# Down products of the experts, and keys, queries and values of pairs three to seven, as three products of rounded halves

## What is computed

```
x = x + tanh(g_xattn[0]) * xattn(layernorm(x), ctx, ctx, Wq, bq, Wk, bk, Wv, bv, Wo, bo)
x = x + tanh(g_ffn[0]) * ffn(layernorm(x), ...)

# xattn
q = Q @ Wq.T + bq;  k = K @ Wk.T + bk;  v = V @ Wv.T + bv      # 16 heads of 16
out = softmax(q k^T / 4) v;  return out @ Wo.T + bo
# ffn
_, topi = top_k(xf @ Wg, 2);  gates = softmax over the two chosen
for e in range(16):
    h = silu(xf @ W1[e] + b1[e]) * (xf @ W11[e] + b11[e])      # 256 -> 512
    y = y + (h @ W2[e] + b2[e]) * gates[:, e, None]            # 512 -> 256
z = silu(xf @ Ws1 + bs1) * (xf @ Ws11 + bs11) @ Ws2 + bs2      # 256 -> 1024 -> 256
```

## Time and profile before

| | us |
|---|---|
| median of 3 runs | 576.16 (576.12 to 580.23) |
| profiled execution, its own time | 570.58 |
| its span | 568.8 |
| PE busy, share of the span | 547.2, 96% |
| POOL busy | 326.7, 57% |

### The profile page before, as it was taken

One profiled execution on the slowest core, in us unless ns is written; L12 is line 12 of the kernel. 1 busy time (PEld: TensorE's weight loads), 2 busy tenths in 40 slices (PEclk: granted clock), 3 DMA queues, 4 the chain that ended last, 5 costly groups with the idle time before them and its releaser, 6 DMA issues.

```text
span 568.8 us, 11908 instructions
## 1 busy us (share of the span) xinstructions
PE 547.2 (96%) x3230; PEld 440.0 (77%) x3231; DVE 340.6 (60%) x846; ACT 238.4 (42%) x787; POOL 326.7 (57%) x267
## 2 busy tenths in 40 slices
PE   8879999999988999988999999999999999999997
PEld 6546666666657878877888888888888888888886
DVE  6556766756668853245555655566555655435687
ACT  0999899999895201202212221122212221233322
POOL 5577798898864286642375575354444650236660
PEclk9999999999999999999999999999999999999999
DMA  8671011011023145245358778557556210013442
GB/s 284 275 294 45 3 39 38 0 37 37 20 76 106 36 157 181 97 130 185 104 182 288 259 268 293 186 177 269 199 197 227 92 46 20 29 57 88 120 123 86
DMA packets 32897, 76.07 MB, mean 134 GB/s; under 512 B 4960, under 2 KB 21856, under 8 KB 29920
## 3 DMA queue, kind: packets, MB, share of 16 engines
q1 hardware_dynamic: 14960, 52.44, 26.1%
q10 hardware_dynamic: 14832, 14.82, 8.2%
q0 software_dynamic: 3072, 8.39, 4.8%
HBM read 54.93 MB, written 18.61 MB: 129 GB/s over the span
## 4 chain that ended last, share of the span: by engine, by line
PE 84%; ACT 7%; DVE 4%; issue 3%; POOL 1%; ACTq 0%; DVEq 0%; POOLq 0%
PE mid L709 14%; PE big L690 8%; PE big L692 8%; PE big L691 8%; PE big L611 5%; PE big L612 5%; PE big L613 5%; PE big L481 4%; ACT arena L797 4%; PE mid L700 4%; PE work L450 3%; PE mid L494 3%; PE work L513 3%; PE last L630 2%; PE last L506 2%
## 5 line engine op out<-in xcount | busy, mean ns | idle before, releaser
L895 ACT ACTIVATE last<-arena 128x512 f32<-128x512 f32 x47 | 28.3, 602 | 183.3 <-DVE arena L1346 183.3
L797 ACT ACTIVATE arena<-big,nmax 128x128 f32<-128x128 f32 x256 | 90.0, 388 | 3.2 <-DVE nmax L1017 3.1
L709 PE MATMUL mid<-dring,arena 128*128 x376 | 89.0, 379 | 0.0
L1346 DVE TENSOR_TENSOR arena<-big,bring 128x512 f32<-128x512 f32 x47 | 32.5, 691 | 88.9 <-PE big L692 88.9
L690 PE MATMUL big<-u_hi,xsT_hi 128*128 x188 | 81.9, 435 | 1.6 <-issue 1.6
L1509 POOL TENSOR_TENSOR u_lo<-arena,u_hi 128x2048 fp32r<-128x2048 f32 x16 | 74.3, 4642 | 1.3
L709 PEld LDWEIGHTS mid<-dring,arena 128*128 128x128 f32 x376 | 67.8, 190 | 7.3
L692 PE MATMUL big<-u_hi,xsT_lo 128*128 x188 | 73.5, 391 | 0.0
L691 PE MATMUL big<-u_lo,xsT_hi 128*128 x188 | 73.4, 391 | 0.0
L1485 POOL TENSOR_TENSOR arena<-arena,rinv 128x1024 f32<-128x1024 f32 (+1 forms) x32 | 58.6, 1832 | 23.1 <-DVE rinv L1025 23.0
L1595 POOL TENSOR_TENSOR pool_mark<-mhalf 128x1 f32<-128x1 f32 x15 | 2.9, 193 | 102.8 <-PE big L692 86.6
(11 more groups left out here) (173 smaller groups left out, 1141.2 us busy)
## 6 DMA issues: line engine op xcount, KB each, us to landing
arena<-up_w_dram SPq DMA_DIRECT2D x16, 1024.0 KB, 7.6
bring<-expert_bias_dram SPq DMA_DIRECT2D x16, 640.0 KB, 5.3
dring<-down_w_dram SPq DMA_DIRECT2D x18, 512.0 KB, 3.3
sorted_y<-arena ACTq DMA_DIRECT2D x47, 128.0 KB, 1.7
arena<-sorted_x ACTq DMA_DIRECT2D x43, 128.0 KB, 2.1
sorted_x<-dring SPq DMA_DIRECT2D x3, 1536.0 KB, 8.7
arena<-ctx_t_dram ACTq DMA_DIRECT2D x8, 256.0 KB, 2.6
dring<-up_w_dram SPq DMA_DIRECT2D x2, 1024.0 KB, 5.0
```

The source lines that it names most:

```text
L709: i = mm(mid[:, 1, 0:D], gT[:, p, c, :], dring[:, slot, c * D:(c + 1) * D], start=(c == 0), stop=(c == HC - 1))
L797: i = nc.scalar.activation(probs[:, u % 2, h, :], big[:, u % 2, h // 4, (h % 4) * CTX:(h % 4 + 1) * CTX], ACT.Exp, bias=nmax[:, u % 2, h:h ...
L1346: v.tensor_tensor(hb1[:, p, :], big[:, p, 0, :], bring[:, slot, 0:HID], ALU.add).then_inc(h1_ready, 1)
```

## The change

The down product of a block becomes twelve fp32r matmuls instead of four fp32 ones. ACT's copy now gives the rounded hidden values, and a new instruction of DVE, `keep_hidden`, the rest of them; PE waits for both. The down weights of each expert are rounded by POOL into `e_down`, with two slots, that lies over the memory of `gshT`. POOL's list for item i is now: mark and up weights as before, then a wait for the last down product of item i - 2, a second mark, and the down weights (`split_down`). Its loop is written out.

Keys, queries and values of pairs 3 to 7 become twelve fp32r matmuls each instead of four fp32 ones. Their weights are rounded once by POOL in pairs 0 and 1 (`split_projection`). The context is rounded by DVE (`round_context`, `keep_context`), the normed input too (`copy_xnT` is two instructions). The context is loaded one slot sooner, into two buffers in turn. PE turns the normed input ahead of the scores of slot 3, no longer behind them.

```diff
 
         ARENA = 16128
-        arena = sb("arena", [P, ARENA])
+        with nc.sbuf_tensor("arena", [P, ARENA], F32) as whole:
+            arena = whole
+        e_down = sb("e_down", [P, 2, 2, DCOLS], F32R)
+        gT_hi = sb("gT_hi", [P, 2, HC, P], F32R)
+        gT_lo = sb("gT_lo", [P, 2, HC, P], F32R)
+        sb("arena_rest", [P, ARENA - 4 * DCOLS - 4 * HID])
         taken = [0]
 
...
+        wr_hi, wr_lo = [u[:, 1, 0:WR].rearrange("p (w c n) -> p w c n", w=3, c=DC) for u in (u_hi, u_lo)]
+        ctx_hi, ctx_lo = [u[:, 1, WR:UCOLS].rearrange("p (c n) -> p c n", c=DC) for u in (u_hi, u_lo)]
+        xnT_hi, xnT_lo = xsT_hi[:, :, :], xsT_lo[:, :, :]
...
+            def rounded(j):
+                return not isinstance(j, int) or j >= ROUNDED
+
+            def project_rounded(w, hi, lo, done):
+                for m in range(DC):
+                    for c in range(DC):
+                        bank = work[:, m * 2 * P:(m + 1) * 2 * P]
+                        w_hi, w_lo = wr_hi[:, w, c, m * P:(m + 1) * P], wr_lo[:, w, c, m * P:(m + 1) * P]
+                        mm(bank, w_hi, hi[:, c, :], start=(c == 0), stop=False)
+                        mm(bank, w_hi, lo[:, c, :], start=False, stop=False)
+                        i = mm(bank, w_lo, hi[:, c, :], start=False, stop=(c == DC - 1))
+                i.then_inc(done, 1)
...
             def project_k(j):
-                pe.wait_ge(ctx_loaded, 16 * j + 16)
-                project(1, ctxT_1 if isinstance(j, int) and j == 1 else ctxT, k_ps, work)
+                if rounded(j):
+                    pe.wait_ge(ctx_split, j - ROUNDED + 1)
+                    project_rounded(1, ctx_hi, ctx_lo, k_ps)
+                else:
+                    pe.wait_ge(ctx_loaded, 16 * j + 16)
+                    project(1, ctxT_1 if j == 1 else ctxT, k_ps, work)
...
             def project_v(j, bank=work, halves=range(2)):
                 src = ctxT_1 if isinstance(j, int) and j == 1 else ctxT
                 for b in halves:
                     for c in range(DC):
-                        i = mm(bank[:, b * D:(b + 1) * D], src[:, c, b * CTX:(b + 1) * CTX], wqkvo[:, 2, c, :],
-                               start=(c == 0), stop=(c == DC - 1))
+                        o, rows = bank[:, b * D:(b + 1) * D], slice(b * CTX, (b + 1) * CTX)
+                        if rounded(j):
+                            mm(o, ctx_hi[:, c, rows], wr_hi[:, 2, c, :], start=(c == 0), stop=False)
+                            mm(o, ctx_hi[:, c, rows], wr_lo[:, 2, c, :], start=False, stop=False)
+                            i = mm(o, ctx_lo[:, c, rows], wr_hi[:, 2, c, :], start=False, stop=(c == DC - 1))
+                        else:
+                            i = mm(o, src[:, c, rows], wqkvo[:, 2, c, :], start=(c == 0), stop=(c == DC - 1))
...
+                    if behind and ahead2 and u == 3:
+                        pe.wait_ge(xfT_ready, j)
+                        project_xnT(j + 2)
                     if u < 2:
                         scores(j, u + 2)
                     elif ahead:
@@ -547,8 +593,8 @@
                     if ahead and behind and u == 2:
                         pe.wait_ge(qT_ready, DC * j + 2 * DC)
                         project_v(j + 1)
-                    if ahead2 and u == 3:
-                        pe.wait_ge(xfT_ready, j) if behind else pe.wait_ge(qT_ready, DC * j + 2 * DC)
+                    if ahead2 and not behind and u == 3:
+                        pe.wait_ge(qT_ready, DC * j + 2 * DC)
                         project_xnT(j + 2)
...
+            pe.wait_ge(w_split, 3)
...
             def down(b, p):
-                slot = pe.snap(item_of(b) % WSLOTS)
+                item = item_of(b)
+                slot = pe.snap((item + 1) % 2)
+                pe.wait_ge(e_split, item)
                 pe.wait_ge(gT_ready, b + 1)
                 if not (isinstance(b, int) and b < 1):
                     pe.wait_ge(y_ready, b)
                 for c in range(HC):
-                    i = mm(mid[:, 1, 0:D], gT[:, p, c, :], dring[:, slot, c * D:(c + 1) * D], start=(c == 0), stop=(c == HC - 1))
+                    w_hi, w_lo = e_down[:, slot, 0, c * D:(c + 1) * D], e_down[:, slot, 1, c * D:(c + 1) * D]
+                    mm(mid[:, 1, 0:D], gT_hi[:, p, c, :], w_hi, start=(c == 0), stop=False)
+                    mm(mid[:, 1, 0:D], gT_hi[:, p, c, :], w_lo, start=False, stop=False)
+                    i = mm(mid[:, 1, 0:D], gT_lo[:, p, c, :], w_hi, start=False, stop=(c == HC - 1))
                 i.then_inc(down_ps, 1)
...
-            def load_context(j):
-                act.wait_ge(v_ps, j)
-                act.dma_start(ctxT, ctx_t[j]).then_inc(ctx_loaded, 16)
-
-            def pair(j, ahead, ahead2, behind, behind2):
+            def load_context(j, slot):
+
+                act.wait_ge(k_ps, j)
+                act.dma_start(ctxT_1 if slot else ctxT, ctx_t[j]).then_inc(ctx_loaded, 16)
+
+            def pair(j, slot, ahead, ahead2, behind, behind2):
                 for u in range(UNITS):
+                    if u == 1 and ahead2:
+                        load_context(j + 2, slot)
                     copy_probs(j, u)
                     if behind2 and u == 0:
                         round_xfT(j - 2)
...
-                    if u == 2 and ahead2:
-                        load_context(j + 2)
...
-                nc.scalar.activation(gT[:, p, :, :].rearrange("p c n -> p (c n)"), mid[:, 0, :], ACT.Copy).then_inc(gT_ready, 1)
+                nc.scalar.activation(gT_hi[:, p, :, :].rearrange("p c n -> p (c n)"), mid[:, 0, :], ACT.Copy).then_inc(gT_hi_ready, 1)
...
+                if isinstance(j, int) and j < ROUNDED:
+                    v.tensor_copy(xnT.rearrange("p c n -> p (c n)"), bank[:, :]).then_inc(xnT_ready, 1)
+                    return
+                v.tensor_copy(xnT_hi.rearrange("p c n -> p (c n)"), bank[:, :]).then_inc(xnT_hi_done, 1)
+                dve.wait_ge(xnT_hi_done, j - ROUNDED + 1)
+                v.tensor_tensor(xnT_lo.rearrange("p c n -> p (c n)"), bank[:, :], xnT_hi.rearrange("p c n -> p (c n)"),
+                                ALU.subtract).then_inc(xnT_ready, 1)
+
+            def round_context(j, slot):
+                dve.wait_ge(ctx_loaded, 16 * j + 16)
+                v.tensor_copy(ctx_hi, ctxT_1 if slot else ctxT).then_inc(ctx_hi_done, 1)
+
+            def keep_context(j, slot):
+                dve.wait_ge(ctx_hi_done, j - ROUNDED + 1)
+                v.tensor_tensor(ctx_lo, ctxT_1 if slot else ctxT, ctx_hi, ALU.subtract).then_inc(ctx_split, 1)
...
                         ln1_stats(j + 2, 1)
                     if ahead and behind and u == 2:
                         copy_v(j + 1, 1 - slot)
+                    if behind and ahead2 and u == 2:
+                        round_context(j + 2, slot)
                     if behind and u == 2:
                         copy_xfT(j - 1)
+                    if behind and ahead2 and u == 2:
+                        keep_context(j + 2, slot)
...
+                    if s == 4 and c == 0:
+                        dve.wait_ge(down_ps, BLOCKS - 1)
+                    if s == 5 and c == 0:
+                        dve.wait_ge(down_ps, BLOCKS)
...
+            def keep_hidden(b, p):
+                dve.wait_ge(gT_hi_ready, b + 1)
+                v.tensor_tensor(gT_lo[:, p, :, :].rearrange("p c n -> p (c n)"), mid[:, 0, :],
+                                gT_hi[:, p, :, :].rearrange("p c n -> p (c n)"), ALU.subtract).then_inc(gT_ready, 1)
...
                 if ahead:
                     hidden(n + 1, 1 - p)
+                keep_hidden(n, p)
                 add_out_bias(n - 1, 1 - p)
...
+            def split_projection(n, before):
+                g.tensor_copy(wr_hi[:, n], wqkvo[:, n]).then_inc(w_hi_done, 1)
+                pool.wait_ge(w_hi_done, before + 1)
+                g.tensor_tensor(wr_lo[:, n], wqkvo[:, n], wr_hi[:, n], ALU.subtract).then_inc(w_split, 1)
...
+                    if isinstance(j, int) and j == 0 and u == 2:
+                        pool.wait_ge(k_w_loaded, 16)
+                        split_projection(1, 0)
+                    if isinstance(j, int) and j == 1 and u == 0:
+                        pool.wait_ge(q_w_loaded, 16)
+                        split_projection(0, 1)
+                    if isinstance(j, int) and j == 1 and u == 2:
+                        pool.wait_ge(v_w_loaded, 16)
+                        split_projection(2, 2)
...
+            def split_down(i, before, slot):
+                source = dring[:, i % WSLOTS, :]
+                g.tensor_copy(e_down[:, slot, 0, :], source).then_inc(e_hi_done, 1)
+                pool.wait_ge(e_hi_done, before + 1)
+                g.tensor_tensor(e_down[:, slot, 1, :], source, e_down[:, slot, 0, :], ALU.subtract).then_inc(e_split, 1)
+
+            pool.wait_ge(w_odd, 32)
+            pool.wait_ge(z_ps, 3 * GROUP)
+            split_down(1, 0, 0)
             pool.wait_ge(raw_even, 16)
```

(21 more changed lines are left out.)

32 lines of the change are left out of this document (23 added, 9 removed).

## The result

The changed kernel takes **580.6 us** (median of 20 runs, 578.6 to 585.0). The kernel before takes 576.1 beside it (20 runs, 573.6 to 580.2). The ratio is 1.0083 (95% interval 1.0067 to 1.0098), so the change costs 0.8%. The forecast was 563.1 us with a range of 557.5 to 571.0. It is wrong, 17.5 us too low and with the wrong sign.

A forecast was written before the change was run, and what follows sets the result against it. The prediction took PE to bound the experts' stage and part of the attention. Down products 14.1 us, less 3.1 for POOL's list, plus 2.1 for projections made 13.1 us: 576.2 becomes 563.1 us, range 557.5 to 571.

The forecast's parts named there:

- PE's queue: Expert slots: PE's queue would set up the down product 1.1 us ahead after a later `y_ready`; costed at nothing.
- The third rival: Expert slots: PE's queue or `y_ready` comes late, 0.15 us per slot, 6.8 us lost over 45 slots, 568.5 us; 12%.
- Rounding item 1's down weights puts item 2's up weights back from 249 to about 257 us: POOL ahead of the experts: PE wants those up weights only after 267, so the delay was costed at nothing.
- The hold: Attention: DVE's `keep_context`, two operands in SBUF, slowed beside POOL; 1.20 us where 512 columns take 0.69.
- Down products: Experts: twelve fp32r matmuls take 1.43 us instead of 1.73, 0.30 less; 47 blocks give 14.1 us at most, slot 4.82.
- POOL's list: Experts: POOL needs 10.39 us per item against two slots of 9.64; PE waits before items 5 to 8, 3.1 us back.
- `blk_end`: POOL's list in the experts: the read of `blk_end` is done by a queue working ahead, costed at nothing.
- Projections: Attention: 0.30 us each; keys of pairs 3 to 7 give 1.5 us, pair 7's queries and values 0.6, together 2.1.
- the second rival: The attention gives nothing: `keep_context` beside POOL costs 0.5 us per pair, five pairs lose 2.5, 565.6 us; 20%.
- Medians: Whole kernel: profiled time of 570.6 us becomes 557.5, the median stays 5.6 us above it; clock stays at 2.4 GHz.

The follow-up runs named there:

- both_fixed: items_ahead with DVE's four small gate instructions moved from ahead of the experts to the tail; 562.9 us, ratio 0.9821 to the kernel before.
- short_list: both_fixed with POOL's second subtraction on down weights cut from 1024 to 128 columns from expert 3 on; 559.2 us, ratio 0.9755 to the kernel before.
- experts_fixed: Only the experts' part of the change, with the load and gate moves of both_fixed, attention as before; 567.0 us, ratio 0.9883 to the kernel before.
- before_again: The kernel before, unchanged, run for a second profile; 575.9 us, ratio 0.9992.
- attention_only: Only the attention part of the change, experts as in the kernel before; 576.1 us, ratio 0.9995 to the kernel before.
- items_ahead: Changed kernel with both item loads moved ahead of the transposes and each slot ending with its up product; 570.3 us, ratio 0.9883 to the kernel before.
- both_again: both_fixed run once more, unedited; 562.0 us, ratio 0.9841 to the kernel before.
- after_extra_load: Changed kernel with one more unused load of the block's item ahead of each up product's own; 591.1 us, ratio 1.0317 to the kernel before.
- before_extra_load: The kernel before with one more unused load of the block's item ahead of each up product's own; 575.5 us, ratio 1.0054 to it.

## Why the prediction was wrong, point by point

- **PE's queue, costed at nothing: the step that failed.** "It fits ... I take that to be enough and cost it at nothing; this is the term I trust least." The third rival had the place and the kind of loss, at 12% and 0.15 us per slot. It put the loop over `y_ready` at some 6.7 us where PE has 6.9. It measured 7.14, and PE has 6.76 from the same point; the 6.9 counted from the end of a record, 0.16 us late. The wait that counts was another one, `gT_ready` ahead of the transposes, which `keep_hidden` puts 3.65 us behind the up product. `y_ready`, 0.34 us later, found the queue still busy. Behind it I had 2.2 us, the two times 1.1 of the rival. The queue takes 3.5: 1.0 from `keep_hidden`'s end to the down product's first register instruction, with the item's load of 0.30 in it, and 2.5 from there to the up product. The earlier trace rows showed only the down product's own register instructions; I gave the loads beside them no cost. The loss is 0.30 us per slot on average, just what the down product gives. Moving the loads gives back **11.5 us**, less than 45 times 0.30, since POOL's waits then show in full.
- **"Rounding item 1's down weights puts item 2's up weights back from 249 to about 257 us", costed at nothing.** The shift was right (258.1) and PE did have its weights. What was not asked is what DVE does in those 8 us. The hold was in the prediction, but for the attention alone and only for instructions with two operands in SBUF: **3.6 us** by the ratios, 4.6 in the profiles, of which 1.7 are the lower clock behind the wait. The prediction took the clock to stay at its 2.4 GHz level.
- **Down products, 0.30 us each.** Right: 4.84 us per slot once the queue is out of the way; 4.82 was predicted.
- **POOL's list.** Right in mechanism, and nearly in place: PE waits mostly at the first blocks of items 5 and 7 (slots of 6.34 and 5.96 us in both_fixed), with 0.3 at 6 and 8. Mis-sized, 4.2 us instead of 3.1. In the changed kernel it shows in part only (slots 10 and 14 take 5.88 us, some 0.4 more than the longest of the others around them), because slots of 5.13 us leave POOL 10.27 for its 10.39.
- **`blk_end`.** Right: POOL's lists follow one another without a gap, so the load costs nothing there. The same kind of load on PE decides everything, as PE has to pass waits right ahead of it.
- **Projections, 2.1 us.** Pairs in the loop shorten by 0.3 as said. Pair 2 gives 0.9 back, and about 1 us is left, between the forecast and the second rival. That rival's mechanism, a hold of `keep_context` by POOL, is there in every pair from 3 to 7 (1.16 to 1.26 us, as in the earlier trace rows), yet the looped pairs shorten; what costs, by the argument above, is the cast ahead of it, once.
- **The rest.** 11.5 + 3.6 are 15.1 of the 17.5 us. POOL's 1.1 and the projections' 1.1 leave 0.2. That it closes so well is luck, as the first two terms are good to some 2 us each. The sum behind both_fixed (1 - 0.9773 predicted, 1 - 0.9821 and 1 - 0.9841 measured) closes to within 0.7% of the time.
- **Medians.** That the clock would stay at 2.4 GHz held in the profiles of before, short_list and experts_fixed; in before_again, attention_only, items_ahead, both_again and the changed kernel the clock from 20 to 40 us was 0.76 to 0.94. That it weighs on both kernels alike is assumed.
- **Open.** In the changed kernel's profile the tail is 2.0 us longer, with a stall of DVE of 3.06 us at 560 in it whose releaser isn't shown; items_ahead has none. Why up product 3 comes so late in the changed kernel (1.46 us more than before, 0.17 in items_ahead) was not followed past its wait of 0.62. Why the gap is 0.48 and not 0.22 where the loop jumps back isn't shown either; in items_ahead it is gone too. The +1.9 us from 180 to 240 were not followed. None of these was tested.

## What to carry to other kernels

When an engine's work gets shorter, follow its queue and not only its operands: from the last wait it must pass, over every register load behind it, to the instruction that is due, and compare that loop with the engine's own work over the same span, two slots if it spans two. Put loads behind queued work, never between a wait and what is due. When work on POOL is moved, look at what DVE does in the new place: here an instruction of 16 columns was held for 4.40 us, until POOL's of 4.65 had ended.

## What the runs showed of the hardware

- A load of a register from SBUF takes 0.30 us on PE's queue. One more of them cost 0.34 us per slot in after_extra_load, and nothing in the slots from block 4 on in before_extra_load, where the queue was ahead.
- DVE instructions with all operands in SBUF (cast, tensor_scalar, tensor_tensor) and POOL's tensor instructions excluded each other until the first had ended: 0.16 and 0.23 us became 1.16 and 4.40. Those with an operand in PSUM kept their 0.69 and 0.42 us.
- A kernel that is otherwise the same was 4.0 us later at 40 us in the execution whose clock was 0.76 from 20 to 40 us than in the one where it was 1.00. Where the clock was 0.71 to 0.72, a shared group took 3.56 us instead of 1.89.
